# Softmax denominators inverted in fp32, split into two fp32r parts and spread over partitions by one-pass fp32r matmuls

## The reference

```python
q = (x @ wq_w.T + wq_b).reshape(b, t, 32, 32)
k1 = x @ wk_w.T + wk_b;  v1 = x @ wv_w.T + wv_b          # one head of 32
scores = einsum('bqhd,bkd->bhqk', q, k1) / sqrt(32)      # causal
weights = softmax(scores)
attn = einsum('bhqk,bkd->bqhd', weights, v1) @ wo_w.T + wo_b
x = layernorm(x + attn)
x2 = clip(x * 448/max|x|, -448, 448);  w2 = clip(w * 448/max|w|, -448, 448)
x = layernorm(x + x2 @ w2 * (1/scales))
```

## Time and profile before

| | |
|---|---|
| median of 3 runs | 2719.75 us (2717.81 to 2719.91) |
| the profiled execution | 2719.72 us, its span 2718.0 us |
| PE busy | 2542.1 us, 94% of the span |
| DVE busy | 1879.0 us, 69% |
| ACT busy | 1273.5 us, 47% |
| POOL busy | 865.6 us, 32% |
| mean granted TensorE clock | 0.974 |

### The profile page before, as it was taken

One profiled execution on the slowest core, in us unless ns is written; L12 is line 12 of the kernel. 1 busy time (PEld: TensorE's weight loads), 2 busy tenths in 40 slices (PEclk: granted clock), 3 DMA queues, 4 the chain that ended last, 5 costly groups with the idle time before them and its releaser, 6 DMA issues.

```text
span 2718.0 us, 45333 instructions
## 1 busy us (share of the span) xinstructions
PE 2542.1 (94%) x15400; PEld 1588.6 (58%) x15400; DVE 1879.0 (69%) x1432; ACT 1273.5 (47%) x1571; POOL 865.6 (32%) x569
## 2 busy tenths in 40 slices
PE   7999998889999999999878999999999997799998
PEld 5888885545544444444544555444444445688887
DVE  6343336668788889999555788888899993444444
ACT  2222224545566666777334565666777670100000
POOL 2321302433322222212334333222221223566663
PEclk9999998989999999999888999999999998899999
DMA  7343334411211111011233122111101104122221
GB/s 232 124 145 141 116 128 141 122 40 51 62 45 39 39 40 40 12 39 40 67 95 94 44 66 51 40 39 39 40 29 37 39 1 162 48 85 90 88 93 62
DMA packets 75076, 197.24 MB, mean 73 GB/s; under 512 B 8559, under 2 KB 8559, under 8 KB 72815
## 3 DMA queue, kind: packets, MB, share of 16 engines
q1 hardware_dynamic: 50220, 140.52, 17.9%
q10 hardware_dynamic: 24768, 55.59, 5.3%
HBM read 123.72 MB, written 72.35 MB: 72 GB/s over the span
## 4 chain that ended last, share of the span: by engine, by line
PE 62%; issue 7%; DVE 5%; ACT 5%; POOL 3%; DMA 1%; ACTq 1%; SPq 0%; DVEq 0%; POOLq 0%
PE bank L1165 16%; PE bank L1177 15%; PE bank L1153 13%; PE bank L1261 13%; ACT prob L689 4%; DVE acc L940 3%; PE bank L1195 2%; POOL prob L546 2%; PE bank L1187 2%; DMA q_st<-max_d 1%; PE bank L1250 1%; DVE acc L937 1%; POOL att_lo L538 0%; ACT att_hi L700 0%; DVE r_den L901 0%
## 5 line engine op out<-in xcount | busy, mean ns | idle before, releaser
L689 ACT ACTIVATE prob<-bank 128x1024 f32<-128x1024 f32 (+3 forms) x1280 | 1077.4, 897 | 627.6 <-PE bank L1165 595.2
L940 DVE TENSOR_TENSOR acc<-acc,prob 128x2048 f32<-128x2048 f32 (+3 forms) x512 | 1093.4, 2136 | 131.1 <-POOL prob L546 85.8
L1165 PE MATMUL bank<-q_st,keys 98*128 98x512 f32 (+3 forms) x2560 | 712.5, 392 | 88.6 <-ACT prob L689 63.0
L1165 PEld LDWEIGHTS bank<-q_st,keys 98*128 98x128 f32 x2560 | 427.6, 192 | 391.6 <-ACT prob L689 308.3
L1177 PE MATMUL bank<-prob,v_t 128*32 128x512 f32 (+3 forms) x5120 | 596.6, 548 | 11.1 <-POOL prob L546 11.1
L546 POOL TENSOR_SCALAR_AFFINE_SELECT prob<-prob 128x512 f32<-128x512 f32 x256 | 300.8, 1179 | 873.0 <-ACT prob L689 872.4
L1075 PE MATMUL bank<-xt_hi,w_hi 128*128 128x512 f32 x576 | 227.3, 395 | 16.4 <-DVE xt_lo L777 15.7
L1075 PE MATMUL bank<-xt_hi,w_lo 128*128 128x512 f32 x576 | 226.6, 393 | 0.0
L1075 PE MATMUL bank<-xt_lo,w_hi 128*128 128x512 f32 x576 | 226.2, 393 | 0.0
L1177 PEld LDWEIGHTS bank<-prob,v_t 128*32 128x32 f32 x5120 | 107.9, 109 | 197.8 <-issue 141.4
L1261 PE MATMUL bank<-wf_hi,xs_hi 128*128 128x512 f32 x512 | 202.8, 396 | 0.0
(11 more groups left out here) (118 smaller groups left out, 2668.7 us busy)
## 6 DMA issues: line engine op xcount, KB each, us to landing
q_st<-q_hi_d SPq DMA_DIRECT2D x128, 256.0 KB
xt_raw<-x_t SPq DMA_DIRECT2D x16, 1024.0 KB, 6.9
q_hi_d<-part_hi ACTq DMA_DIRECT2D x64, 256.0 KB, 2.1
q_lo_d<-part_lo ACTq DMA_DIRECT2D x64, 256.0 KB, 2.3
q_st<-q_lo_d SPq DMA_DIRECT2D x64, 256.0 KB
x<-x_d SPq DMA_DIRECT2D x32, 512.0 KB, 3.2
out<-y ACTq DMA_DIRECT2D x32, 512.0 KB, 2.6
res<-x SPq DMA_DIRECT2D x24, 512.0 KB, 4.0
```

Source lines behind the costliest of these rows:

```text
L689: nc.scalar.activation(prob[:, t % SLOTS, 2 * p:2 * p + 2, off:NB], bank[:, 2 * p:2 * p + 2, off:NB], ACT.Exp, scale=SCALE).then_inc(p_don ...
L940: nc.vector.tensor_tensor(acc[:, r, :, off:NB], acc[:, r, :, off:NB], new, ALU.add).then_inc(acc_done, 1)
L1165: last = nc.tensor.matmul(bank[:, h, off:NB], keys[:, b * JB + t // QT, t % QT * P:(t % QT + 1) * P], q_st[:, slot, h, off:NB], start=True ...
```

## The change

The reciprocal stays as it is. Two instructions are added behind it in `invert`: a copy to fp32r (`r_hi`, the upper part in all eight rows), and a multiply-add with a per-partition scalar `r_lower`, which is 0 in the first four of each eight equal rows and -1 in the last four, so that `r_parts` holds r_den in the first four (rounded to fp32r as it is written) and the remainder r_den - r_hi in the last four. `spread` gets a second 1 per column, four rows further down, and becomes fp32r: each of its matmuls now adds an upper and a lower part. It is built in a piece of `kv` that is free at that time and then copied. ACT waits for that copy before it writes that piece of `kv`, near the end of the first part.

```diff
-    FIXED = 4 + HG
+    FIXED = 6 + HG
...
-        spread = sb("spread", [P, QT, P])
+        spread = sb("spread", [P, QT, P], F32R)
+        r_lower = sb("r_lower", [P, 1])
...
             r_den = sb("r_den", [P, P], F32, s)
-            s.enter_context(nc.sbuf_tensor("wo_stage_rest", [P, 2 * D - P], F32))
+            r_hi = sb("r_hi", [P, P], F32R, s)
+            r_parts = sb("r_parts", [P, P], F32R, s)
+            s.enter_context(nc.sbuf_tensor("wo_stage_rest", [P, 2 * D - 3 * P], F32))
...
-            nc.gpsimd.memset(spread[:], 0.0).then_inc(fixed, 1)
+            nc.gpsimd.memset(kv[:, TB - 1], 0.0).then_inc(fixed, 1)
...
+            pool.wait_ge(fixed, 3 + HG)
+            nc.gpsimd.affine_select(out=kv[:, TB - 1].rearrange("p (g d) -> p g d", d=HD), in_=kv[:, TB - 1].rearrange("p (g d) -> p g d", d=HD),
+                                    compare_op=ALU.not_equal, fill=1.0, base=-(REPS // 2), pattern=[[-REPS, QT * HG], [0, HD]], channel_multiplier=1).then_inc(fixed, 1)
+            pool.wait_ge(fixed, 4 + HG)
+            nc.gpsimd.tensor_copy(spread[:].rearrange("p c n -> p (c n)"), kv[:, TB - 1]).then_inc(fixed, 1)
...
+            act.wait_ge(fixed, FIXED - 1)
             add_bias(TB - 1, G, 0)
...
+            dve.wait_ge(consts, 6)
+            nc.vector.tensor_reduce(r_lower[:], ident[:].rearrange("p (a s i) -> p a s i", s=2, i=REPS // 2)[:, :, 1], AX.XY, ALU.add).then_inc(lower_rows, 1)
+            dve.wait_ge(lower_rows, 1)
+            nc.vector.tensor_scalar(r_lower[:], r_lower[:], -1.0, None, ALU.mult).then_inc(lower_rows, 1)
...
-                nc.vector.reciprocal(r_den[:], bank[:, DEN_BANK, 0:P]).then_inc(den_read, 1)
+                nc.vector.reciprocal(r_den[:], bank[:, DEN_BANK, 0:P]).then_inc(den_inverse, 1)
+                dve.wait_ge(den_inverse, 2 * n + 1)
+                nc.vector.tensor_copy(r_hi[:], r_den[:]).then_inc(den_inverse, 1)
+                dve.wait_ge(den_inverse, 2 * n + 2)
+                nc.vector.scalar_tensor_tensor(out=r_parts[:], in0=r_hi[:].bitcast(F32), scalar=r_lower[:], in1=r_den[:], op0=ALU.mult, op1=ALU.add).then_inc(den_read, 1)
...
-                        last = nc.tensor.matmul(bank[:, DEN_BANK, c * P:(c + 1) * P], spread[:, c], r_den[:], start=True, stop=True)
+                        last = nc.tensor.matmul(bank[:, DEN_BANK, c * P:(c + 1) * P], spread[:, c], r_parts[:], start=True, stop=True)
```

More of the change, by code:

```diff
@@ L225, in build @@
         den_read = sem("den_read")
+        den_inverse = sem("den_inverse")
+        lower_rows = sem("lower_rows")
         spread_done = sem("spread_done")
@@ L487, in _ @@
                 nc.gpsimd.memset(head_col[:, h, h * REPS:(h + 1) * REPS], 1.0).then_inc(fixed, 1)
-            nc.gpsimd.affine_select(out=spread[:].rearrange("p c (h d) -> p (c h) d", d=HD), in_=spread[:].rearrange("p c (h d) -> p (c h) d", d=HD),
+            nc.gpsimd.affine_select(out=kv[:, TB - 1].rearrange("p (g d) -> p g d", d=HD), in_=kv[:, TB - 1].rearrange("p (g d) -> p g d", d=HD),
                                     compare_op=ALU.not_equal, fill=1.0, base=0, pattern=[[-REPS, QT * HG], [0, HD]], channel_multiplier=1).then_inc(fixed, 1)
+            pool.wait_ge(fixed, 3 + HG)
+            nc.gpsimd.affine_select(out=kv[:, TB - 1].rearrange("p (g d) -> p g d", d=HD), in_=kv[:, TB - 1].rearrange("p (g d) -> p g d", d=HD),
+                                    compare_op=ALU.not_equal, fill=1.0, base=-(REPS // 2), pattern=[[-REPS, QT * HG], [0, HD]], channel_multiplier=1).then_inc(fixed, 1)
+            pool.wait_ge(fixed, 4 + HG)
+            nc.gpsimd.tensor_copy(spread[:].rearrange("p c n -> p (c n)"), kv[:, TB - 1]).then_inc(fixed, 1)
             def inverse_deviation(moments, done, before):
@@ L875, in _ @@
             dve.wait_ge(wo_cut, KT)
+            dve.wait_ge(lower_rows, 2)
             dve.wait_ge(flag_ready, 1)
```

## The result

The changed kernel takes 2729.90 us (median of 6 runs, 2723.69 to 2734.06), beside 2719.83 us for the kernel before in the same job: ratio 1.0035, 95% interval 1.002 to 1.005. It is slower by 10.1 us. The forecast was 2729. The profiled execution of the changed kernel is the fastest of its six, 2723.69 us, 6.2 us under the median; its trace shows where the time lies, and sizes that rest on a few us are taken from medians of several runs.

The account below looks back on a forecast made before the run. The prediction took a chain of TensorE (62% PE) to bound the kernel. Its terms, -10.8 + 2.4 - 1.0 + 8.4 + 10.2 = +9.2 us on 2719.75, gave 2729 us, range 2712 to 2740.

Parts of the forecast that it names:

- The sum: Whole kernel: all terms together make it 9.2 us slower, so 2729 us.
- the collision: Stage 1, six groups r = 0: POOL's subtraction L538 holds the added DVE instructions, PE 1.4 us late each, +8.4 us.
- the clock: Behind the six stage 1 gaps PE's clock drops to 0.50, costing 1.7 us each, +10.2 us, bounds 0 and +20.
- Saving on PE: Spread matmuls at L1195: four fp32r matmuls take 0.52 us instead of 0.97, saving 0.45 us a group.
- The added instructions: DVE behind the reciprocal: cast 217 ns, multiply-add 291 ns; with waits, r_parts is 0.60 us later than r_den.
- Groups r = 1 and r = 0: 24 groups r = 1 gain 0.45 us each (-10.8); 16 groups r = 0 without collision lose 0.15 each (+2.4).
- Stage 0 and the end: Nine groups a batch, both kinds plus a path through DVE's clipping and SP's store: -0.5 us a batch, -1.0 in all.
- The preparation: At the start, an added mask, copy and two tiny reductions cost nothing, being covered; about 1 us without that cover.
- Stage 1: Stage 1 is longer by 4 to 12 us in each batch, stages 2 and 3 shorter by 1 to 3 each.

Follow-up runs that it names:

- PE's part alone: Changed kernel with the reciprocal writing r_parts directly as fp32r, cast and multiply-add removed, lower part left out: 2701.92 us, ratio 0.9931 to the kernel before.
- PSUM operands: Changed kernel with the inverse kept in PSUM, where the cast and the multiply-add read it: 2713.20 us, ratio 0.9975 to the kernel before.
- experiment 2: Changed kernel with nine unused 512-column matmuls filling PE's wait for r_parts in stage 1's groups r = 0: 2721.22 us, ratio 1.0011 to the kernel before.
- experiments 4 and 5: Changed kernel with the cast written as the maximum of r_den with itself (4: 2736.16 us) or as a tensor_reduce over a length-1 axis (5: 2732.24 us).
- POOL later: Changed kernel with POOL's stage 1 subtraction waiting for the multiply-add of the inverses in the same group: 2720.34 us, ratio 1.0002 to the kernel before.
- e_before_early: Kernel before the change, with the reciprocal moved ahead of DVE's addition for key tile 2: 2707.09 us, ratio 0.9953.

## Why the prediction was right

**The sum** was +9.2 us, measured +10.1. The mechanism was right in its main step, the collision and the clock behind it. That the number came within 1 us is luck in part: without the collision the change gives -6.5 us where the sum has -9.4, and the collision with its clock costs 16.6 where the sum has 18.6. The two errors have opposite signs. Its parts:

- **Saving on PE,** 0.45 us a group: 0.42 (0.92 to 0.50). Over 64 groups that is 27 us, of which PE's part alone kept 17.9.
- **The added instructions.** The cast was put at 217 ns and takes 227, the multiply-add at 291 and takes 352 where nothing holds it. The interpolation over columns missed that a multiply-add on 128 columns stands well above it. r_parts is 0.65 us after r_den instead of 0.60: an error of 0.05, and the 0.29 us to spare in r = 1 survived it.
- **Groups r = 1 and r = 0,** forecast -1.8 + 0.6 = -1.2 us for 8 groups of stage 2 or 3: measured -0.9 and -0.9 in stage 2, -1.6 and -2.2 in stage 3. With PSUM operands it is -3.4 over the four, where the sum has -4.8: right in kind, somewhat too much.
- **The collision,** named with its six places: right in all six. r_parts was to be ready 2.98 us after r_den (654.7 - 651.72) and was 2.82 to 3.01. POOL's subtraction took 2.34 to 2.35 us at all six. The mask behind it did get in between the two added instructions, and the multiply-add took 0.62 us for 0.35; the 0.27 is just what taking the middle (654.7 for 654.43) allowed for it. The delay, without the clock, was forecast at 8.4 us and experiment 2 leaves 8.0 at most, by the estimate there 6 to 8.
- **The clock,** forecast at 10.2 us, 1.7 for each gap, from low stretches of stage 0: the filled gap gives 8.6 at least and some 11 by the estimate there. The size was a choice between 0 and 3.4 us a gap, and the runs don't measure it finer. In the trace of the changed kernel the stretches are longer than taken, mostly 6.8 us; in the two kernels of experiments 4 and 5 they are mostly the 3.4 us that the prediction took. A low clock behind a gap is not sure either: five of six here, six of six in each of those two.
- **Stage 0 and the end,** -1.0 us: wrong as far as the traces tell. In the five traces in which stage 0 is alike but for how the two parts are made (the changed kernel, PSUM operands, POOL later, maximum, reduce) stage 0 is -1.2 to +2.9 us in the first batch and -0.3 to +2.1 in the second, on average +1.7 and +0.9. They are set against a single trace of before, so the size is rough. Together with the 1.4 us of stages 2 and 3, it more than accounts for the 2.9 us between -9.4 and -6.5; stage 1 gives some of it back (-2.2 and -2.1 with PSUM operands, -1.8 by the sum). Why stage 0 gains nothing is open.
- **The preparation,** put at nothing: no cost can be seen. The first exponential starts at 452.5 us before the change, at 453.7 in the changed kernel, and at 453.8 in e_before_early, which has no preparation.
- **Stage 1** was to be longer by 4 to 12 us in each batch: 7.6 in the first, 3.1 in the second, a little under. In the second batch the third gap had no low stretch behind it, and the second one a short one. Stages 2 and 3 were to be shorter by 1 to 3 us: 0.9 to 2.2.

## What to carry to other kernels

A small instruction on the path between two engines is priced by who else is running when it starts, not by its mean: look up, for each place where it will stand, what GpSimd does at that moment. Moving one of the two in time, POOL later or DVE earlier, only changed the loser here, and PE waited for the masks instead. What ended it was to keep in PSUM what the copy reads, and one of the multiply-add's two inputs. The same instruction off that path, stalled for as long, cost nothing measurable. And a gap of TensorE costs twice, once as time and once in the clock behind it: here some 6 to 8 us and 9 to 11 us over six gaps.

## What the runs showed of the hardware

- A DVE copy or an instruction with two SBUF inputs was held by POOL's subtraction on SBUF that had started first: 128x128, from a median of 227 ns to 2318 (copy), 292 to 2402 (maximum), 352 to 2081 (multiply-add). With its input in PSUM the cast takes 290 to 292 ns, with one input in PSUM the multiply-add 347 to 349, and a tensor_reduce on one SBUF input 285 to 289, at every place.
- It works in both directions: POOL's subtraction took 3.81 to 4.09 us behind DVE's addition in e_pool_later, instead of 2.35.
- An fp32r matmul of 128x128 over 128 columns goes in one record where fp32 goes in two; four with their loads take 0.52 us against 0.97. The price per record is the same, 0.12 to 0.13 us.
- Nine matmuls without use in each of six gaps of 2.6 to 2.9 us kept the clock at 1.00 behind them and were worth 8.6 us or more in all.
